# Moving the second half of the softmax and the statistics in VectorE's step of two cross attention phases

## What is computed

```
# L0 (phase A0, then F0)
Q = q @ Wq.T + bq;  K = k @ Wk.T + bk;  V = k @ Wv.T + bv      # 16 heads of width 8
scores = einsum('bhqd,bhkd->bhqk', Q_, K_) / 8 ** 0.5
scores = where(causal, scores, -1e9)
att = einsum('bhqk,bhkd->bhqd', softmax(scores), V_)
att_h = layer_norm(att + q, ln_g, ln_b)
x = gelu(att_h @ W1.T + b1) @ W2.T + b2 + att_h
# L2 (phase A2, then F2)
scores = einsum('bqhd,bkhd->bhqk', q, k);  scores = where(mask == 0, -1e20, scores)
attn = softmax(scores / sqrt(128));  out = einsum('bhqk,bkhd->bqhd', attn, v)
x = layernorm(out @ w_out + b_out + query, g1, beta1)
```

## Time and profile before

| | |
|---|---|
| median of 3 runs | 2589.75 us (2586.35 to 2591.84) |
| the profiled execution | 2593.18 us, of it the span 2591.4 us |
| PE busy | 2355.9 us (91%) |
| DVE busy | 1894.2 us (73%) |
| ACT busy | 1498.3 us (58%) |
| POOL busy | 1539.6 us (59%) |
| A0's loop, about 69 to 386 us | a step 6.14 us, a lap's last-to-first one 6.43 us |
| A2's loop, about 1077 to 1380 us | a step 5.87 us, a lap's last-to-first one 6.13 us |

### The profile page before, as it was taken

The page is one execution under the profiler, slowest core; times in us unless marked ns, Lnnn a source line. Parts: engine busy times, 40 slices in busy tenths (PEclk is TensorE's granted clock), DMA queues, the critical chain, the costliest instruction groups (busy, mean ns, idle before and its releaser), DMA issues. The chain is left out here.

```text
span 2591.4 us, 83416 instructions
## 1 busy us (share of the span) xinstructions
PE 2355.9 (91%) x26926; PEld 1806.6 (70%) x26926; DVE 1894.2 (73%) x4003; ACT 1498.3 (58%) x3407; POOL 1539.6 (59%) x2438
## 2 busy tenths in 40 slices
PE   6999998987777777999998988999999999999899
PEld 4666666975656565777776876777777777777587
DVE  4676764139999994677776667888888888888566
ACT  4777775558888884777776542444444444444333
POOL 2555555127888884455556776666666666666332
PEclk9999999989999997999999998999999999999999
DMA  4111111235555551222121223333333333333111
GB/s 121 38 38 39 36 40 44 71 109 153 148 155 148 154 153 39 51 46 46 47 47 41 65 63 83 92 94 97 97 95 95 94 94 96 94 94 93 50 58 54
DMA packets 443043, 211.78 MB, mean 82 GB/s; under 512 B 206400, under 2 KB 433856, under 8 KB 442816
## 3 DMA queue, kind: packets, MB, share of 16 engines
q1 hardware_dynamic: 442944, 210.51, 30.7%
HBM read 113.36 MB, written 29.88 MB: 55 GB/s over the span
## 5 line engine op out<-in xcount | busy, mean ns | idle before, releaser
L666 PE MATMUL bank<-sb_ident,sb_region 128*77 128x128 f32 x3072 | 413.8, 278 | 85.7 <-ACT sb_pT L754 84.8
L666 PEld LDWEIGHTS bank<-sb_ident,sb_region 128*77 128x77 f32 x3072 | 350.2, 151 | 139.9 <-issue 137.7
L754 ACT ACTIVATE sb_pT<-bank 77x1024 f32<-77x1024 f32 x384 | 391.6, 1020 | 67.1 <-PE bank L666 67.0
L858 DVE TENSOR_REDUCE sb_max<-bank 128x8 f32<-128x616 f32 x256 | 203.5, 795 | 205.8 <-PE bank L648 118.0
L1528 ACT ACTIVATE sb_l<-sb_l 128x640 f32<-128x640 f32 x128 | 94.5, 738 | 386.2 <-DVE sb_l L1576 386.2
L749 ACT ACTIVATE sb_region<-sb_region 128x616 f32<-128x616 f32 x384 | 276.8, 721 | 1.4 <-POOL sb_region L995 1.4
L1649 POOL TENSOR_TENSOR sb_pn<-sb_l,sb_r_all 128x512 f32<-128x512 f32 x128 | 134.7, 1052 | 233.4 <-DVE sb_r_all L1586 229.5
L1398 PE MATMUL bank<-sb_region,sb_wqkv 128*128 128x128 f32 x2048 | 255.2, 279 | 1.6 <-DVE sb_region L1564 0.8
L682 PE MATMUL bank<-sb_pT,sb_v 77*32 77x128 f32 x6144 | 248.2, 279 | 3.6 <-ACT sb_pT L754 3.2
L1438 PE MATMUL bank<-sb_wvo,sb_region 128*64 128x512 f32 x1024 | 248.0, 605 | 0.0
L1398 PEld LDWEIGHTS bank<-sb_region,sb_wqkv 128*128 128x128 f32 x2048 | 243.6, 195 | 4.1 <-DVE sb_region L1564 1.5
(11 more groups left out here) (183 smaller groups left out, 5645.4 us busy)
## 6 DMA issues: line engine op xcount, KB each, us to landing
sb_region<-in_side SPq DMA_DIRECT2D x64, 616.0 KB, 3.8
sb_pT<-sb_region SPq DMA_DIRECT2D x512, 64.0 KB, 2.1
sb_kF<-sb_region SPq DMA_DIRECT2D x512, 64.0 KB, 2.1
scratch_after_A<-sb_y SPq DMA_DIRECT2D x256, 64.0 KB, 1.8
sb_fx<-scratch_after_A SPq DMA_DIRECT2D x96, 128.0 KB, 2.1
sb_mask<-in_mask SPq DMA_DIRECT2D x64, 154.0 KB, 2.2
sb_x<-scratch_after_F SPq DMA_DIRECT2D x128, 64.0 KB, 1.9
sb_ctx<-in_ctxT SPq DMA_DIRECT2D x192, 38.5 KB, 1.9
```

What stands on the lines that cost most here:

```text
L666: mm = nc.tensor.transpose(two[0:C, h * T:(h + 1) * T], p_s[b.par][:, head * C:(head + 1) * C], ident[:])
L754: nc.scalar.activation(pT_s[k][:], two[0:C, :], ACT.Copy).then_inc(pT_kept.sem(b), 1)
L858: nc.vector.tensor_reduce(dst, by_bank_and_head(scores_half(k)), AX.X, ALU.max).then_inc(max_made.sem(b), 1)
```

## The change

In A0 and A2, DVE's step calls the same functions in another order. `peak` and `shift` of the second half stand right behind those of the first, ahead of `invert`, `normalise` and `sums`. `sum_context(b+1)` goes from the beginning of the step to behind `sums`. `statistics(b-3)` at the beginning of step b becomes `statistics(b-2)` at the end of it, which is the same batch one step earlier in the numbering and the same place between the neighbours. `aggregate` stays. PE, ACT, POOL and SP have the same instructions and waits in the same order.

```
             def step(b, has):
-                if has(1) and ph == "A0":
-                    sum_context(b + 1)
-                if has(-3):
-                    statistics(b + -3)
                 if has(1):
                     peak(b + 1, 0)
                 if has(-3):
                     aggregate(b + -3)
                 if has(1):
                     shift(b + 1, 0)
+                    peak(b + 1, 1)
+                    shift(b + 1, 1)
                 if has(-1):
                     invert(b + -1)
                     normalise(b + -1)
                 if has(-2):
                     sums(b + -2)
-                if has(1):
-                    peak(b + 1, 1)
-                    shift(b + 1, 1)
+                if has(1) and ph == "A0":
+                    sum_context(b + 1)
                 if has(2) and ph == "A2":
                     key_bias(b + 2)
+                if has(-2):
+                    statistics(b + -2)
```

## The result

The changed kernel takes 2614.93 us in the median of four executions (2612.8 to 2617.05), the kernel before 2590.8 us beside it; the ratio is 1.0092, 95% interval 1.0078 to 1.0106. Run once more on another occasion, with five executions, it took 2611.41 against 2591.03 us, ratio 1.0077 (1.0063 to 1.0091). It is slower by 20 to 24 us.

The account below looks back on a forecast made before the run. PE's in-order program and its few waits were taken to bound the kernel. Delays at L616 summed to 24.1 us, less 2.6 for hidden register instructions: 2589.75 + 21.5 = 2611.3 us, range 2598 to 2622.

Parts of the forecast that it names:

- The second half gains nothing: DVE's second shift comes 0.9 us earlier, but neither PE at L645 nor ACT's `exps(b+1, 1)` starts earlier: gain 0.
- the rival that took it for a wait for that shift: Idle 0.20 us ahead of L645 is a wait for the second half's shift; faster, 2586 or 2574 us; chance 0.03.
- The normalisation becomes the last: DVE's chain to PE's L616: 3.74 us against 3.54 in an ordinary A0 step, 3.67 in A2; PE waits there.
- The lower bound: Signal may leave before L915's record ends, delays 0.08 us less, 5 us more register work hidden: about 9 us remain.
- The price of a step: Wait at L616: A0 0.20 us ordinary, 0.31 in a lap's first two; A2 0.07 and 0.27; laps 1.02 and 0.68.
- The delay stays in full: PE's work behind L616 and the next scores start later, so each delay is added to the period once a step.
- one sign that the prediction named: In the changed kernel's trace, DVE's idle time before the first L858 in A0 would be shorter per step.
- 2.6 us off for PE's register instructions, hidden in the new wait: PE's register instructions before L645 and L620 run while L616 waits: 0.05 us off a step, 52 steps.
- The sum: A0 13.3, A2 8.8, written-out steps 0.8, 0.6 and 0.6: 24.1 us, less 2.6 for registers, 21.5 us.
- The context sum: In A0 `sum_context(b+1)` ends later, SP's context load issues 0.9 to 1 us later; cost 0 unless loads take 3.6 us.
- `sums(b-2)` costs 0 in A2: `attend(b, 0)` waits for `sums(b-2)`, ending 0.2 us after `o_made`; L616 and L612 between take longer, so cost 0.
- the one with 0.80 us instead of 0.72 behind a shift: DVE waits 0.80 instead of 0.72 us at two places a step: 17.6 us on top, 2629 us; chance 0.03.

Follow-up runs that it names:

- The kernel with only the wait moved: Changed kernel, but in A0 L693's transposes write into bank 7 and PE asks for the normalisation at L682: 2597.81 against 2591.03 us before, ratio 1.003.

## Why the prediction was right, step by step

- *The second half gains nothing.* Right. The kernel with only the wait moved is back at A0's old lap and no lower, although its shift is 0.9 us earlier. The idle time of 0.20 us ahead of L645 stands in the changed kernel's ordinary steps too, with the shift earlier, so the rival that took it for a wait for that shift is out.
- *The normalisation becomes the last.* Right, in both phases, with the hand-over as priced: 0.05 to 0.06 us from the end of L915's record to L616, so the signal does not leave early. The lower bound rested on a misreading: the `o_made` that L927 waits for is that of the batch before (it reads `sb_o1` while L915 writes `sb_o0`), so its start 0.21 us behind L915 says nothing of this signal. (Its terms also leave 7.9 us, not 9.)
- *The price of a step.* A0: 0.17 and 0.18 in the ordinary steps (0.20 foreseen), 0.30 and 0.35 in a lap's first two (0.31 for both), 1.00 a lap for 1.02. The chain is 3.71 to 3.72 for 3.74: L908 to L915 is 0.28 for 0.29, and the rest is rounding; the pitch behind L863 is 0.72 as foreseen. A2: 0.04 twice, 0.29 and 0.22, 0.59 a lap for 0.68; my short cut to price a lap's second step like the first was 0.05 too much here.
- *The delay stays in full.* Right: laps grew by the sum of the single delays. But one sign that the prediction named has it the wrong way round: DVE's idle time ahead of the first L858 of A0 was to get shorter, and it got longer (1.46 us in an ordinary step before, 2.00 after), as it must when DVE does the same work in a longer step.
- *2.6 us off for PE's register instructions, hidden in the new wait.* Wrong. A0's lap grew by all that the chain overshot, and L645 behind a lap's branch still starts after 0.41 us of idle time put down to issue:

```profile
218.66 0.11 PEld L645 LDWEIGHTS bank<-sb_causal,sb_identb 128*128 128x128 bf16 x2 [0.41 <-issue]
```

- *The sum.* Foreseen 21.5 us, measured in the two phases 20.4; the median moved by 24.1 and, in the second comparison, 20.4 us. The number is nearer than its terms, and that is luck. The laps were 1.4 us too dear (A0 13.3 for 13.0, A2 8.8 for 7.7). The steps written out were priced at 2.0 us, and what the whole phases show beside their laps is -0.3 us, nothing clear of the scatter. Against these 3.7 us too much stood the 2.6 us taken off for PE's registers, which were not there.
- *The context sum.* Right: SP's load of the context moved from 0.36 us ahead of L616 to 0.58 behind it, and in A0's loop L620 never waits for it, before or after. Over the whole program L620 waited for it three times before and four times in the changed kernel, all in the first steps of A0 and A1 (us, times; before, then changed):

```profile
  DMA sb_ctx<-in_ctxT: 13.8, 3
```

```profile
  DMA sb_ctx<-in_ctxT: 14.3, 4
```

- *`sums(b-2)` costs 0 in A2.* Right for this change, but said too lightly. It was the next appointment in line, and the run with the normalisation alone put back met it.

Of the rivals, the one with 0.80 us instead of 0.72 behind a shift is out: the second L858 starts 0.71 us after L863, whose record is 0.80 long, in the very place of the change. The Trainium skill (VectorE: DVE Perf Modes, The DRAIN you can't avoid) has the next operation wait until the pipeline is empty, and adds that one that is not held starts earlier. The prediction left that half out, so the page does not speak for the 0.80; by these rows the next operation starts 0.08 us before the first one's record ends.

## What to carry to other kernels

In a software pipeline read each hand-over as an appointment: when it is ready, and when the other engine asks. Work moved ahead is worth nothing if its reader has slack, and is free for the work behind it only up to that work's own slack (in an ordinary step of A0 0.72 us more was free and 1.54 us cost 0.18 a step). When a move is taken back in part, check the appointment next in line too; and a wait that guards a bank can often be put where its slack is, by choosing another bank.

## What the runs showed of the hardware

A DVE operation that works from SBUF to SBUF can be held by POOL. The key bias took 0.19 us where nothing held it and 0.69 to 0.75 us when it started just behind a POOL operation of 0.70 us, and ended 0.06 us behind that operation each time, while the POOL operation kept its length. In the changed kernel the key bias is held too (median 0.39 us), where PE doesn't wait for it. It happened in A0 with the residual sum too, whose two inputs are in SBUF there, already in the kernel before and more in the changed one; before and after (the second block is of the changed kernel):

```profile
L927 DVE TENSOR_TENSOR sb_t<-sb_o,sb_xb x64: 281/292/429, 37.4 to 425.9; 128x128 f32<-128x128 f32 x64
```

```profile
L927 DVE TENSOR_TENSOR sb_t<-bank,sb_xb x128: 277/278/293, 599.1 to 1442.5; 128x128 f32<-128x128 f32 x128
L927 DVE TENSOR_TENSOR sb_t<-sb_o,sb_xb x64: 279/357/661, 38.0 to 438.8; 128x128 f32<-128x128 f32 x64
```

With one input in PSUM, in A1 and A2, it keeps its 0.28 us; with both in SBUF its median went from 0.29 to 0.36 us, as it now starts beside POOL's block of keys (0.70 us) and not beside L1001 (0.46 us); where it is longer than 0.29 us it ends 0.15 us behind that operation, before and after. It cost nothing there, since PE in A0 doesn't wait for it. Not every DVE operation is held: the context sum (L895, 0.22 us) and the statistics (L931, 0.28 us), with one input, keep their lengths beside POOL's operations.

The other direction shows as well. In the kernel before, POOL's `centre` starts in 59 of A0's 64 steps 0.02 to 0.27 us behind the residual sum, while that is still running, and takes 0.83 to 0.93 us; in the other five it takes 0.80. In the changed kernel it never starts beside that sum in A0 and takes 0.80 throughout (shortest, median, longest in ns; before, then changed):

```profile
L1011 POOL TENSOR_SCALAR sb_z<-sb_t,sb_mv,sb_rstd x128: 794/803/933, 43.7 to 1423.3; 128x128 f32<-128x128 f32 x128
```

```profile
L1010 POOL TENSOR_SCALAR sb_z<-sb_t,sb_mv,sb_rstd x128: 794/801/804, 43.7 to 1446.4; 128x128 f32<-128x128 f32 x128
```

The Trainium skill (SBUF — State Buffer, Who interferes with whom) says that DVE and GpSimd share one pair of SBUF ports, that whichever operation issues first has it for its whole length, and that a DVE operation in a two-port mode needs it, or one with two SBUF inputs beside a GpSimd operation that reads SBUF; the lengths here agree, in both directions, with the one difference that the held operation's record doesn't start later but is longer. Whether the key bias ran in such a mode no run here shows.
